# Filter stage of a two-layer recurrent block: TensorE's program as a loop of ten turns with fixed operands, channels copied by ScalarE, ranks in five matmuls

## The reference

```python
xn = layernorm(x); s = attention(xn)      # 16 heads, full softmax
g = silu(ffn(xn)); x = x + s * g          # gated FFN with int8 weights
xn = layernorm(x); s = filter(xn)         # one causal filter of 512 taps per channel
g = silu(moe(xn)); x = x + s * g          # 8 experts, the best 2 for each token
def moe(x):
    v, i = top_k(x @ router_w.T, 2); w = softmax(v)
    return sum(w[k] * expert[i[k]](x) for k in (0, 1))
```

## Time and profile before

| | |
|---|---|
| median of 3 runs | 1512.23 us (1511.62 to 1512.91) |
| the profiled execution's own time | 1508.08 us |
| its span | 1506.3 us |
| PE busy | 1309.6 us, 87% of the span |
| DVE, ACT, POOL busy | 997.9, 868.9, 554.0 us |
| `layer0` | from the start to about 993.7 us of the span |
| filter stage | 993.7 to about 1179.4 us |
| `experts`, `combine` | from 1179.4 us |

### The profile page before, as it was taken

One profiled execution on the slowest core, in us unless ns is written; L12 is line 12 of the kernel. 1 busy time (PEld: TensorE's weight loads), 2 busy tenths in 40 slices (PEclk: granted clock), 3 DMA queues, 4 the chain that ended last, 5 costly groups with the idle time before them and its releaser, 6 DMA issues. The chain is left out here.

```text
span 1506.3 us, 29415 instructions
## 1 busy us (share of the span) xinstructions
PE 1309.6 (87%) x8092; PEld 669.3 (44%) x8092; DVE 997.9 (66%) x2343; ACT 868.9 (58%) x1661; POOL 554.0 (37%) x543
## 2 busy tenths in 40 slices
PE   5899999999999999999989998657884599999970
PEld 2433433434343343343433334234432488888770
DVE  1878888888888888888867885234443254444448
ACT  0277787788778778778867875212221244444332
POOL 2122342342343234224224215355555244444440
PEclk9999999999999999999989998779996799999995
DMA  6333222312312322231231232368773223222229
GB/s 222 105 97 111 91 73 73 107 55 70 107 55 74 110 92 72 71 108 55 70 108 52 75 94 68 94 219 282 254 245 99 77 71 90 78 65 66 62 58 334
DMA packets 116391, 162.27 MB, mean 108 GB/s; under 512 B 17874, under 2 KB 52370, under 8 KB 116051
## 3 DMA queue, kind: packets, MB, share of 16 engines
q1 hardware_dynamic: 103842, 137.73, 28.2%
q0 software_dynamic: 8448, 17.58, 3.4%
q10 hardware_dynamic: 4016, 6.05, 1.3%
HBM read 104.20 MB, written 49.77 MB: 102 GB/s over the span
## 5 line engine op out<-in xcount | busy, mean ns | idle before, releaser
L775 DVE TENSOR_REDUCE row_max<-ps_max 128x2 f32<-128x1024 f32 x512 | 614.9, 1219 | 137.2 <-PE ps_max L1032 133.5
L983 ACT ACTIVATE probs<-ps_exp 128x512 f32<-128x512 f32 x1024 | 556.3, 597 | 132.1 <-PE ps_exp L1032 114.1
L1032 PE MATMUL ps_exp<-q_op,k_op 32*128 32x512 f32 x1024 | 352.3, 502 | 26.9 <-ACT probs L983 19.9
L1032 PEld LDWEIGHTS ps_exp<-q_op,k_op 32*128 32x128 f32 x1024 | 145.9, 184 | 410.1 <-ACT probs L983 368.8
L1113 PE MATMUL ps_y<-probs,v_aug 128*32 128x512 f32 x2048 | 279.0, 617 | 0.2 <-ACT y_raw L989 0.2
L1032 PE MATMUL ps_max<-k_op,q_op 32*128 32x512 f32 x1024 | 255.4, 498 | 2.6 <-DMA k_op<-k_parts_scratch 1.6
L1579 ACT ACTIVATE hidden<-ps_h,b 128x256 f32<-128x256 f32 x268 | 118.7, 474 | 157.4 <-PE ps_h L1553 147.0
L1622 POOL DMA_INDIRECT y_scratch<-result,goes_to x134 | 128.4, 958 | 154.7 <-DVE result L1607 128.6
L671 POOL TENSOR_TENSOR rstd<-var_eps,minus_half 128x4 f32<-128x4 f32 x32 | 32.8, 1026 | 366.5 <-DVE var_eps L770 366.5
L315 POOL DMA_INDIRECT sorted_scratch<-rows,place x120 | 116.1, 967 | 88.8 <-issue 31.7
L1560 PE MATMUL ps_o<-w,hidden 128*128 128x128 f32 x1072 | 131.3, 276 | 0.0
(11 more groups left out here) (185 smaller groups left out, 1483.8 us busy)
## 6 DMA issues: line engine op xcount, KB each, us to landing
q_op<-q_parts_scratch SPq DMA_DIRECT2D x16, 1024.0 KB, 5.7
k_op<-k_parts_scratch SPq DMA_DIRECT2D x16, 1024.0 KB, 8.4
q_op<-k_pad_scratch SPq DMA_DIRECT2D x15, 1024.0 KB
k_op<-k_pad_scratch SPq DMA_DIRECT2D x15, 1024.0 KB
unit_rows<-sorted_scratch SPq DMA_DIRECT2D x136, 66.0 KB
q_parts_scratch<-qk_split SPq DMA_DIRECT2D x16, 512.0 KB, 3.1
k_parts_scratch<-qk_split SPq DMA_DIRECT2D x16, 512.0 KB, 2.9
q_parts_scratch<-qk_split SPq DMA_DIRECT2D x16, 256.0 KB, 2.4
```

Of the source, the lines that this page charges most:

```text
L775: dve.tensor_reduce(row_max[group // 2][:, t, head:head + 2], ps_max[u][:, :, :], AX.X, ALU.max)\
L983: act.activation(probs[s % 2][:, i, :], ps_exp[i % 2][:, :], ACT.Exp).then_inc(exp_done, 1)
L1032: return pe.matmul(out, lhsT, rhs, start=True, stop=True)
```

## The change

- PE's program of the filter stage is a loop of ten turns (`nc.Fori`), a turn for one batch (4 to 13) and three groups. Only semaphore counts depend on the turn; they are computed in registers. All operands are fixed: there are three Toeplitz buffers, three picks buffers, three by_time buffers, three PSUM banks of each kind, and one xn_now and one xnT_now.
- So that operands can be fixed, ACT copies each group's four channels out of xn_all into a picks buffer (`pick`, 128x256) and each batch into xn_now (`take`, 128x512).
- Batches 14 and 15 and groups 30 and 31 follow behind the loop, the products after both batches. The first turn turns a group that doesn't exist: ACT fills its by_time buffer, and the semaphores start at offsets.
- ACT fetches rows one batch ahead: `fetch_rows(b + 1)` ends turn b.
- `rank_tokens` becomes five matmuls of 40 to 8 columns. ps_s and ps_rank share a bank, so that `score(b)` also waits for `placed` of the batch before.
- SP issues the loads of the experts' first weights after load 6 and no longer after load 3.
- In `layer0`, ACT waits for `inverse_spread` ahead of the first two Toeplitz loads.

```diff
-TOEPS = 4
+TOEPS = 3
+PER_BATCH = 3
+TRAIL = 2
...
-    return ops[q % 2][1 - q // 2 % 2][:, :, :].bitcast(FP32)
+    return ops[q % TOEPS % 2][1 - q % TOEPS // 2][:, :, :].bitcast(FP32)
...
-        for t in range(TT):
-            pe.matmul(ps_rank[:, t, :], before[:, 0, :], hot_both[:, t, :], start=True, stop=(t == 0))
-            for u in range(t):
-                pe.matmul(ps_rank[:, t, :], before[:, 1, :], hot_both[:, u, :], start=False, stop=(u == t - 1))
-        for t in range(TT):
-            last = pe.matmul(ps_rank[:, TT, :], before[:, 1, :], hot_both[:, t, :], start=(t == 0), stop=(t == TT - 1))
+        pe.matmul(ps_rank, before[:, 0, :], hot_both[:, :, :], start=True, stop=False)
+        for behind in range(1, TT + 1):
+            last = pe.matmul(ps_rank[:, behind:, :], before[:, 1, :], hot_both[:, 0:TT + 1 - behind, :], start=False, stop=(behind == TT))
...
             act.wait_ge(k_stored, 32)
+            act.wait_ge(inverse_spread, 16 * B)
             for q in range(2):
                 load_toep(act, dram, route, ops, q)
...
-                if q == TOEPS - 1:
+                if q == 2 * TOEPS:
                     weights.load_biases(sp, dram)
...
+            def pick(q):
+                if q < NQ:
+                    wait(act, convolved, q - 2)
+                    channels = res.xn[:, :, CG * q:CG * q + CG].rearrange("p (m u) c -> p c u m", u=2)
+                    act.activation(picks[q % 3][:, :, :, :], channels, ACT.Copy).then_inc(picked, 1)
+            def take(b):
+                act.activation(xn_now[:, :, :], res.xn[:, TT * b:TT * b + TT, :], ACT.Copy).then_inc(now_ready, 1)
...
+            for b in looped:
+                q = quads(b)[0]
+                if b > ROUTED:
+                    route.copy_x(act, banks, b)
+                    take(b + 1)
+                reverse(q)
+                pick(q + 3)
+                route.exp(act, b)
+                reverse(q + 1)
+                pick(q + 4)
+                reverse(q + 2)
+                pick(q + 5)
+                route.fetch_rows(act, res, b + 1)
...
-                        last = pe.matmul(ps_t[p][32 * i:32 * i + 32, 0:T - 128 * u], res.xn[:, u::2, CG * q + i], toep_of(ops, q)[:, i, 128 * u:],
+                        last = pe.matmul(ps_t[p][32 * i:32 * i + 32, 0:T - 128 * u], picks[p][:, i, u, :], toep_of(ops, p)[:, i, 128 * u:],
...
+            with nc.Fori(0, LOOPED, engines=bass.OrderedEngineSet([pe.engine]), hint_back_edge=True) as n:
+                b, q = n + ROUTED, PER_BATCH * n
+                turn_x(b)
+                turn(q - 1, 2)
+                product(q, 0, n + 1)
+                score(b)
+                product(q + 1, 1, n + 1)
+                turn(q, 0)
+                route.rank_tokens(pe, banks, b)
+                product(q + 2, 2, n + 1)
+                turn(q + 1, 1)
+            for b in behind:
+                turn_x(b)
+                if b == behind[0]:
+                    turn(trailing[0] - 1, 2)
+                score(b)
+                route.rank_tokens(pe, banks, b)
+            for q in trailing:
+                product(q, q % 3, q // 3 + 1)
+            for q in trailing:
+                turn(q, q % 3)
```

More of the change, by code:

```diff
@@ L1304, in sem @@
             return ctx.enter_context(nc.semaphore(name))
[L1306 to L1311, removed]
+        by_time = [sb(f"by_time{p}", [128, T]) for p in range(3)]
+        xn_now = sb("xn_now", [128, TT, C])
+        picks = [sb(f"picks{p}", [128, CG, 2, N_TOK // 256]) for p in range(3)]
+        route.use([sb("xnT_now", [128, T])] * 2, [sb(f"rows{k}", [128, TT, ROW])[:, :, :] for k in range(2)])
+        ps_t = [ps(f"ps_t{p}", [128, T]) for p in range(3)]
+        ps_b = [ps(f"ps_b{p}", [128, TT, CG, B, 2]) for p in range(3)]
+        convolved, time_copied, time_turned, whole_out, spread, picked, now_ready = (
+            sem(n) for n in ("convolved", "by_time_copied", "turned", "whole_out", "spread", "picked", "now_ready"))
+        COPIED, TURNED, SPREAD = 3, 1, 4
         units = sb("units", [128, E + 1], INT32)
@@ L1329, in route_and_convolve @@
         batches = range(ROUTED, B)
+        LOOPED = (NQ - TRAIL) // PER_BATCH
+        looped = range(ROUTED, ROUTED + LOOPED)
+        behind = range(ROUTED + LOOPED, B)
+        trailing = range(NQ - TRAIL, NQ)
         def quads(b):
-            n = b - ROUTED
-            return range(NQ * n // len(batches), NQ * (n + 1) // len(batches))
+            return range(PER_BATCH * (b - ROUTED), PER_BATCH * (b - ROUTED) + PER_BATCH)
         def fill(eng, experts):
@@ L1399, in turn, with turn_x @@
                 last.then_inc(time_turned, 1)
[L1401 to L1409, removed]
-                route.score(pe, banks, b)
-                convolve(qs[1])
-                route.rank_tokens(pe, banks, b)
-                for q in qs[2:]:
-                    convolve(q)
-            turn(NQ - 1)
+            def turn_x(b):
+                pe.wait_ge(now_ready, b + 1 - ROUTED)
+                route.turn_x(pe, res, banks, b, xn_now)
@@ L1435, in out @@
                 last.then_inc(spread, 1)
+            dve.sem_inc(spread, SPREAD)
             route.clear(dve, [ROW_SETS - 1])
@@ L1440, in _ @@
             dve.tensor_copy(fill_rows[:, :, C], route.fill_numbers).then_inc(fill_step, 1)
-            for b in batches:
-                qs = quads(b)
-                out(qs[0] - 1)
+            for b in looped:
+                q = quads(b)[0]
+                out(q - 1)
                 route.choose(dve, banks, b)
-                out(qs[0])
+                out(q)
                 route.place_tokens(dve, banks, b)
-                for q in qs[1:-1]:
-                    out(q)
+                out(q + 1)
+            for b in behind:
+                if b == behind[0]:
+                    out(trailing[0] - 1)
+                route.choose(dve, banks, b)
+                route.place_tokens(dve, banks, b)
             def done(ins, n):
@@ L1470, in _ @@
             dve.tensor_copy(units[:, 1:], sums[1][:, :]).then_inc(units_ready, 1)
-            out(NQ - 1)
+            for q in trailing:
+                out(q)
             load_ends(dve)
```

66 lines of the change are left out of this document (39 added, 27 removed).

## The result

The change made the kernel a little slower: 1517.65 us (median of 22 runs, 1509.03 to 1526.26) against 1511.41 us (median of 22 runs, 1505.35 to 1518.03), a ratio of 1.0035 with a 95% interval from 1.0022 to 1.0048. The prediction was 1472.6 us.

A forecast was written before the change was run, and what follows sets the result against it. No engine was full; PE's instructions were taken as late, with POOL's scatters the floor at 10.08 us a batch. Scatters ending 41.6 us earlier, less 2 for starving, gave 1512.2 - 39.6 = 1472.6 us, range 1467 to 1492.

The forecast's parts named there:

- about ten such pieces: Filter stage, PE: stretches with 5.4 us lost, read as late instructions of straight code, taken as gone inside the loop.
- The last scatter ends at 1001.9 + 9 T + 30: Filter stage, POOL: end of the last scatter, with T the time of a turn; each us over 10.08 costs 9 us.
- T = 9.3: PE's loop: a turn's work of 8.8 us plus 0.5 for register instructions and branch, 0.8 under POOL's 10.08.
- Rival 4: PE's loop: stalls stay, caused by full DMA engines or the sequencer; T 14.2 to 14.7, 1508 to 1512 us; chance 0.06.
- Stage's start, -4.6: Start of the filter stage: the last inverse spread lands earlier with the loads behind it, 4.6 us off (3 to 4.9).
- First places, +1.3: First batch of the loop: a take and a turn of a missing group delay the first places 1.3 us (0 to +4).
- Ranks in five matmuls, 0.2: PE's loop: five rank matmuls take 0.2 us a turn, between 0.16 and 0.44.
- Picks, 0.5 each: ACT's turn: three picks of 256 elements at 0.5 us each (0.3 to 0.65), hidden under POOL's 10.08.
- Rows fetched ahead: ACT fetching rows a batch ahead removes POOL's 28.8 us of waits for rows in the filter stage.
- Starving, 2: Filter stage: three Toeplitz buffers and later weight loads starve POOL around the third turn, 2 us (0 to 5).
- rival 1: Filter stage: Toeplitz loads into three buffers become the bound; at T = 11.5, 1483 us (range 1479 to 1492); chance 0.18.
- The 15.6 us after the last scatter: End of the filter stage: the time from the last scatter's end to the next stage stays 15.6 us.

The follow-up runs named there:

- a_double: The changed kernel with every scatter from batch 4 on issued twice, the second time into a scratch table that nothing reads; 1643.95 us in one run.
- a_noload: The changed kernel with only the first three Toeplitz operands loaded and used by all later products (output wrong); 1521.67 us in one run.
- a_straight: The changed kernel with PE's ten turns written out instead of looped; 1.0007 of the time before.
- a_ahead: The changed kernel reordered: PE scores before the product and ranks behind it, DVE places first, POOL's row waits for the batch's last product; 1.0027 of before.
- b_wait: The kernel before with only ACT's wait for inverse_spread added ahead of the first two Toeplitz loads; 0.9965 of the time before.
- a_early_free: The change's buffers, PE's turns written out, ranks placed early in a row, POOL's row waiting for no product; 0.9913 of the time before.

## Why the prediction was wrong

**The step that failed** is "There are about ten such pieces in twelve batches, and I read them as PE's instructions arriving late", and with it "I take the stalls as gone inside the loop". The code fetches did go from the loop, but the pieces stayed, one a turn. In its place the runs showed reports held by POOL's row: doubling the row doubled the hold (a_double), and taking the loads away (a_noload) or writing the loop out (a_straight) changed nothing. I had seen both halves of the clue. ACT waited 62.2 us for a PE that was "remote" while PE's own timeline had the product long finished, and the gap in POOL's scatters, 3.67 us before 1072.30, lies inside that piece. I never asked when POOL's row had begun. The piece's price was mixed, too: over its 8.39 us the granted clock was 0.80, and from 1070 to 1072 us it was 0.50, so part of the 5.4 us was PE at the lower of its two levels and not PE standing.

**The formula held, its input did not.** "The last scatter ends at 1001.9 + 9 T + 30": with T = 14.92 it gives 1166.2, and the trace has 1168.9. Of the 2.7 us between, 2.4 are the first scatter of batch 4 (1004.32 instead of 1001.9). T = 9.3 was a sum of PE's work, and PE is not what closes a turn.

**Rival 4** ("the loop doesn't cure the stalls ... the full DMA engines or the sequencer", T = 14.2 to 14.7, 1508 to 1512 us) was right in its result and wrong in both its causes. It got a chance of 0.06. The evidence I held against it was one 4 us stretch in which PE was busy with full DMA engines. That speaks against the DMA engines, and says nothing of other causes. Even its T was 0.2 to 0.7 too short: after the release the change has DVE move an output (0.9 us) and do the gate arithmetic (0.6 us) ahead of the places, and in before both were done by then, DVE going straight to `taken` at 1070.23. I read this as why the change's turn is longer than before's; the turn of a_ahead, where DVE's places come first, agrees. It makes most of the slowdown: nine turns take 134.3 us (1004.32 to 1138.58) where they took 122.4 (1005.20 to 1127.65), 12 us lost. The last two batches win 6.6 of it back, since they follow at POOL's pace (20.2 us instead of 26.8), and the stretch behind the last scatter loses 3.

**Term by term:**
- Stage's start, -4.6: right. b_wait measured 5.3 (2.9 to 7.7). The profile after shows only 2.7 at the first scatter, because attention's end came 2.0 us later in that execution (971.32 against 969.35).
- First places, +1.3: measured +1.8 (12.6 us after the first scatter instead of 10.8).
- Ranks in five matmuls, 0.2: 1069.12 to 1069.33, 0.21 us, right. Picks, 0.5 each: 0.64, the upper bound; hidden, as said.
- Rows fetched ahead: POOL's wait for rows fell from 28.8 us to one of 5.2, right, and brought nothing, because place was held by the same release. Two waits with one cause can't be saved one at a time.
- Starving, 2: hardly any at turns of 14.9 us (1.9 us of PE's waits for loads in all, and without the loads the turn is no shorter, a_noload). At the turn of 10.1 that the term was made for it was not tried; the versions with early ranks say that it would have been more, and rival 1 stays open.
- The 15.6 us after the last scatter "stay": wrong, 18.6. The row of 24 scatters held the last two products' reports, and also DVE's steps in counting the units. ACT's and PE's timelines after show them working only behind it:

```profile
1172.45 1.09 ACT L1377 ACTIVATE by_time<-ps_t 128x512 f32<-128x512 f32 x2 [23.65 <-remote]
1173.10 1.57 PEld L1443 LDWEIGHTS ps_b<-ident,by_time 128*128 128x128 f32 x8 [18.69 <-ACT by_time L1377]
1173.10 1.97 PE L1443 MATMUL ps_b<-ident,by_time 128*128 128x128 f32 x8 [17.80 <-ACT by_time L1377]
```

Which of them lengthens the stretch was not tried; in a_noload, with the same row of 24, it is 16.3 us.

The range (1467 to 1492) was too narrow because all its cases but two small ones shared the one reading of "issue".

**Open.** What in the chip holds the reports was not found; that POOL's row is the cause is shown, the way is not. No run parts POOL's own work on a scatter from the DMA writes that the scatter sets off. Why the hold starts some 2 to 5 us in was not tried either, nor why two reports inside the row of 24 were let through. A row of eight was never broken into rows of four with a gap at both ends, since at 1.6 us a gap that costs as much as it gives.

## What to carry to other kernels

When an engine waits for another as "remote" and that other one's timeline shows the work finished, look for what runs on a third engine from the start of the wait to its end; here it was POOL. In this kernel a row of eight indirect DMAs on POOL makes most of PE's hand-offs wait until it is over, so hand-offs on the critical path belong in its first 2 us. Before costing a cure, change the suspected cause alone in thought: "issue" says only that the profile shows no cause.

## What the runs showed of the hardware

- PE's semaphore updates came within 0.1 us in the attention loop up to 900 us, where POOL issues no indirect DMA. In rows of eight (1.26 us each) the first ones late by over 2 us were of matmuls that finished 2 to 5 us into the row, in some rows later; they came up to 8.1 us late (b_wait), most of them 1.4 to 2.1 us after the row. In rows of 16 it was up to 18.4 us, and 29 of 48 came 2.7 to 3.2 us after the row (a_double).
- ACT's updates came within 0.1 us in every trace. DVE's did so in rows of eight of before and the change; in other versions single ones, 6 to 10 us into a row, were up to 1.5 us late (a_early_free), and from 11 us into the last long row after the change on eight were 1.0 to 2.5 us late. So it is PE above all, and not PE alone.
- After PE had stood for held reports its granted clock was at the lower of its two levels for a few us. In the trace after, PE stood from 1055.7 to 1058.4, the granted clock was 0.50 from 1060 to 1066, and the product at 1062.58 took 3.21 us, where at 1.00 it takes 1.71.
- ACT's copy of 256 elements a partition in steps of 1 KB (`pick`) took 0.64 us, as long as one of 512 in a row (`take`, 0.63).
